# A two-layer recurrent/attention kernel: opening rearranged, and another fixed order of steps in its five engine plans

## The reference

```python
xn = _layernorm(x)
s = _L0_attn_ref(xn, ...)            # a Mamba block: in_proj, causal conv of 4 taps, x_proj, dt, a scan over time
                                     # with 16 states per channel, out_proj; then layernorm, gelu MLP 256-1024-256
g = _silu(_L0_ffn_ref(xn, ...))      # FP4 (blocks of 16) quantize/dequantize of activations and weights, gated MLP
x = x + s * g
xn = _layernorm(x)
s = _L1_attn_ref(xn, ...)            # attention over the batch dimension (two entries), 16 heads of 16
g = _silu(_L1_ffn_ref(xn, ...))      # three blocks: linear - layernorm - gelu - linear, plus residual; weights are
                                     # 4-bit values times scales, plus a low-rank product (LoRA)
x = x + s * g
```

## Time and profile before

| | us |
|---|---|
| median of 3 runs (1772.78 to 1775.84) | 1775.19 |
| the profiled execution's own time | 1773.16 |
| its span | 1771.1 |
| PE busy | 1542.6 |
| DVE busy | 1560.9 |
| ACT busy | 1436.5 |
| POOL busy | 1255.8 |

### The profile page before, as it was taken

One profiled execution on the slowest core, in us unless ns is written; L12 is line 12 of the kernel. 1 busy time (PEld: TensorE's weight loads), 2 busy tenths in 40 slices (PEclk: granted clock), 3 DMA queues, 4 the chain that ended last, 5 costly groups with the idle time before them and its releaser, 6 DMA issues.

```text
span 1771.1 us, 26229 instructions
## 1 busy us (share of the span) xinstructions
PE 1542.6 (87%) x7512; PEld 1161.8 (66%) x7512; DVE 1560.9 (88%) x2887; ACT 1436.5 (81%) x3076; POOL 1255.8 (71%) x1314
## 2 busy tenths in 40 slices
PE   2576888989899999989999899989899999999875
PEld 1254666767677777767676677767676767677654
DVE  3959999999999999999999999989999999989811
ACT  1376788889898989899898989889898988888632
POOL 2656767677777868687777868687777869687522
PEclk8687899999999999999999999999999999989987
DMA  7111111111111112111111111112111111111100
GB/s 177 49 48 56 52 49 48 54 43 50 53 61 43 54 49 58 51 49 61 37 61 49 48 50 65 42 53 56 37 60 49 48 60 55 40 57 48 31 0 12
DMA packets 68452, 91.58 MB, mean 52 GB/s; under 512 B 15742, under 2 KB 34758, under 8 KB 68310
## 3 DMA queue, kind: packets, MB, share of 16 engines
q1 hardware_dynamic: 68310, 89.91, 16.9%
HBM read 85.17 MB, written 4.72 MB: 51 GB/s over the span
## 4 chain that ended last, share of the span: by engine, by line
POOL 26%; PE 25%; DVE 20%; ACT 14%; issue 12%; DMA 1%; SPq 0%; POOLq 0%; ACTq 0%; DVEq 0%
PE bank L338 10%; POOL drive L795 10%; PE bank L454 6%; DVE unit L959 5%; POOL wide L844 3%; DVE hc L966 3%; PE y_ps L364 2%; POOL wide L849 2%; POOL wide L846 2%; ACT unit L570 2%; ACT hx L549 1%; DVE xc L991 1%; ACT ops L536 1%; PE bank L325 1%; ACT L536 1%
## 5 line engine op out<-in xcount | busy, mean ns | idle before, releaser
L795 POOL TENSOR_TENSOR drive<-wx,rows 128x1024 f32<-128x1024 f32 x256 | 603.6, 2358 | 157.1 <-DVE unit L959 81.9
L959 DVE TENSOR_TENSOR_SCAN unit<-unit,drive 128x512 f32<-128x512 f32 x512 | 616.5, 1221 | 35.7 <-POOL drive L802 25.6
L570 ACT ACTIVATE unit<-dt,aneg 128x254 f32<-128x254 f32 x1024 | 441.8, 468 | 8.0
L966 DVE TENSOR_TENSOR hc<-unit,rows 128x512 f32<-128x512 f32 x512 | 340.6, 683 | 5.6
L364 PE MATMUL y_ps<-ident,hc 128*128 128x128 f32 x2048 | 278.6, 282 | 62.6 <-DVE hc L966 62.6
L364 PEld LDWEIGHTS y_ps<-ident,hc 128*128 128x128 f32 x2048 | 242.1, 145 | 116.2 <-DVE hc L966 75.4
L338 PE MATMUL bank<-w_l,ops 128*128 128x256 f32 x768 | 195.7, 399 | 15.0 <-DVE xc L994 8.9
L338 PEld LDWEIGHTS bank<-w_l,ops 128*128 128x128 f32 x768 | 146.0, 197 | 66.1 <-DVE xc L994 20.5
L570 ACT ACT_TABLE_LOAD x109 | 139.8, 1283 | 1.9
L579 ACT ACTIVATE carry<-unit 128x4 f32<-128x4 f32 x512 | 79.2, 169 | 68.5 <-DVE unit L973 63.9
L454 PE MATMUL bank<-ops,w_f 128*128 128x256 f32 x512 | 115.8, 385 | 11.2 <-ACT ops L536 11.2
(11 more groups left out here) (229 smaller groups left out, 3132.4 us busy)
## 6 DMA issues: line engine op xcount, KB each, us to landing
rows<-rows_scratch SPq DMA_DIRECT2D x256, 256.0 KB, 3.3
x_t<-in_L_attn_x_dram SPq DMA_DIRECT2D x16, 256.0 KB, 3.9
xs<-in_L_attn_x_dram SPq DMA_DIRECT2D x16, 256.0 KB, 3.5
out_dram<-xs SPq DMA_DIRECT2D x16, 256.0 KB, 2.2
w_f<-in_L_attn_ffn_w_dram SPq DMA_DIRECT2D x2, 1024.0 KB
ops<-in_L_ffn_qweights_dram SPq DMA_DIRECT2D x1, 1536.0 KB, 15.6
w_in<-in_L_attn_in_proj_w_dram SPq DMA_DIRECT2D x1, 1024.0 KB, 5.3
hq_t<-attn_in_proj_weight_dram SPq DMA_DIRECT2D x1, 768.0 KB
```

The source lines that it names most:

```text
L570: last = a_.activation(u[:, k * TOK:(k + 1) * TOK].rearrange("p (b t) -> p b t", b=B)[:, :, 1:TC], dt[p][:, g, :].rearrange("p (b t) -> p ...
L795: g_.tensor_tensor(drive[n % 2][:, :, :].rearrange("p (g b) t -> p g b t", b=B), wx[p][:, :, :].rearrange("p g (b t) -> p g b t", b=B), ro ...
L959: v.tensor_tensor_scan(u[:, :], u[:, :], d, 0.0, ALU.mult, ALU.add).then_inc(S["scan_done"], 1)
L966: v.tensor_tensor(hc[n % NPROD][:, 4 * half:4 * half + 4, :].rearrange("p (g b) t -> p g b t", b=B), unit_of(ch, n, half)[:, :].rearrange( ...
```

## The change

1. Nine small loads leave SP's queue and are issued by ACT, on a semaphore of their own, `small_in`; ACT waits for it instead of `front_in`, PE for both.
2. On DVE the lora dequantization moves from behind `round_(1)` to behind `step_of(0)`, ahead of `conv1`.
3. The gate turns are grouped by weight (4 of gate, 4 of up, then down), and PE waits for each weight's `unscale` alone.
4. The five plans hold the same steps in another order. The text looks wholly different because the period's start is put elsewhere on ACT, DVE and SP; aligned, between 15 of SP's 20 and 80 of DVE's 119 steps keep their sequence.

```diff
         load_front = [
             (w_in[:, :, :], in_proj_w.rearrange("(k p) n -> p k n", p=P)),
+        ]
+        load_small = [
             (g1c[:, :], ln1_g.rearrange("(k p) -> p k", p=P)),
...
-        for half in range(2):
-            for k in range(KD):
-                for wi, dst in ((0, w_g), (1, w_u)):
+        for wi, dst in ((0, w_g), (1, w_u)):
+            for half in range(2):
+                for k in range(KD):
...
+                    for dst, src in load_small:
+                        act.dma_start(dst, src).then_inc(small_in, 16)
                 act.wait_ge(c_done, 8)
-                act.wait_ge(front_in, 16 * len(load_front))
+                act.wait_ge(small_in, 16 * len(load_small))
...
-                pe.wait_ge(w_out_done, 3)
                 for n, (dst, parts) in enumerate(gate_turns):
+                    pe.wait_ge(w_out_done, 1 + min(n // 4, 2))
...
                 step_of(0)
-                dve_step(dve, "conv1", 0)
-                round_(0)
-                scale(2)
-                step_of(1)
-                round_(1)
                 dve.wait_ge(lora_in, 16 * len(load_lora))
                 v.tensor_scalar(l_raw, q_raw, 1.0 / 7.5, -1.0, ALU.mult, ALU.add).then_inc(lora_deq, 1)
...
                                 .to_broadcast([P, NLIN * KD * D // QB, QB]), ALU.mult).then_inc(lora_deq, 1)
+                dve_step(dve, "conv1", 0)
+                round_(0)
+                scale(2)
+                step_of(1)
+                round_(1)
                 step_of(2)
```

More of the change, by code:

```diff
@@ L75 @@
 PE_PLAN = """
[L76 to L79, removed]
+    b0a-- kv-- xp sum8- q-- dt0 b0T-- hqT0- dt1 sum9- b0b-- v1-- sum10- sum11- h1T-- hqT1- ctxT-- hqT2- b1a--
+    sum12- b2b--- sum13- dn- b1T-- sum14- sum15- ao-- xqT skip ygT0- ygT1- g00 sum0 g01 op- u00 u01 sum1 g10
@@ L80 @@
+    sum2 b1b-- g11 u10 u11 u2T- sum3 h2T-- f10- sum4 f11- f12- f13- uT+ b2a-- sum5 f2- b2T-- xi0+ sum6 xi1+ z0+
+    xn1T- xi2+ xi3+ sum7 z1+
 """
 ACT_PLAN = """
[L82 to L85, removed]
@@ L86 @@
-    f13- exp6b out5b u+ exp7a b2n-- out6a exp7b out6b exp8a out7a exp8b b2g-- tap0+ tap1+ hn- z0+ xn1- tap2+
-    tap3+ z1+ out7b out8a xc0+ xc1+ exp9a exp9b out8b exp10a b0n- kv- xp+ out9a out9b exp10b exp11a dt0+ out10a
-    exp11b hq0 b0g- aexp- dt1+ out10b v1- dtexp+
+    exp11b- dt0 b0g-- aexp-- hq0- dt1 v1-- dtexp out10b- exp12a- out11a- exp12b- out11b- exp13a- h1-- hq1-
+    out12a- exp13b- out12b- hq2- ctx-- dtln out13a- exp14a- out13b- exp14b- exp15a- first out14a- exp15b- b1n--
+    out14b- exp0a gatec--- gatem- b1g-- out15a- exp0b xq out15b- s1-- exp1a out0a yg0- exp1b yg1- out0b exp2a
@@ L89 @@
+    out1a exp2b g00 g01 out1b exp3a out2a out2b exp3b exp4a opn- g10 xn+ g11 out3a out3b exp4b u2- exp5a out4a
+    exp5b h2-- out4b exp6a f10- f11- xhf+ f12- f13- usave out5a exp6b out5b u+ exp7a out6a exp7b out6b b2n--
+    exp8a out7a exp8b b2g-- tap0+ tap1+ hn- z0+ tap2+ xn1- tap3+ xc0+ out7b out8a exp9a z1+ xc1+ exp9b out8b
+    exp10a b0n- out9a exp10b xp+ out9b kv- exp11a out10a
 """
 POOL_PLAN = """
-    drive14- drive15- b1-- arg fix0 drive0 xout fin--- drive1 drive2 hb1-- drive3 fix1 f+ drive4 op- drive5 j0in
@@ L92 @@
-    hb2-- drive6 s0b- drive7 b2-- drive8 j0out j1in x1- drive9 drive10 diff- j1out b0- hb0- drive11 xin+ drive12
+    drive14- arg drive15- fix0 b1-- drive0 xout fin--- drive1 drive2 f+ fix1 drive3 op- drive4 hb1-- drive5 j0in
+    s0b- hb2-- drive6 j0out drive7 b2-- j1in drive8 x1- drive9 drive10 diff- j1out b0- xin+ drive11 hb0- drive12
     drive13 log+
@@ L95 @@
 DVE_PLAN = """
[L96 to L102, removed]
+    scan14b- hc14a- hc14b- clr14a- scan15a- wx clr14b- hc15a- scan15b- hc15b- xround clr15a- clr15b- yg- scan0a
+    hc0a clr0a scan0b hc0b scan1a clr0b hc1a scan1b clr1a scan2a hc1b hc2a clr1b clr2a scan2b op- hc2b ug0 clr2b
+    scan3a scan3b hc3a hc3b clr3a scan4a clr3b h2-- hc4a scale0 ug1 scan4b hc4b clr4a scan5a clr4b hc5a scan5b
+    clr5a scale1 round0 hc5b scan6a hc6a clr5b b2s-- scan6b hc6b clr6a scan7a clr6b scan7b hc7a hc7b clr7a
+    xscale+ clr7b x1- scan8a conv0+ scan8b hc8a hc8b clr8a conv1+ round1 b0s- scan9a clr8b hc9a scan9b clr9a
+    scan10a hc9b clr9b hc10a clr10a scan10b scan11a score- scan11b hc10b hc11a f++ attn- clr10b h1- clr11a hc11b
+    scan12a clr11b hc12a scan12b clr12a hc12b scan13a clr12b scan13b hc13a clr13a b1s- hc13b clr13b dt+ scan14a
 """
 SP_PLAN = """
-    rows8- rows11- load+ rows10- rows12- rows13- wr rows14- rows15- rows0 rows1 rows3 rows2 store--- rows4
-    again- rows6 rows5 rows9 rows7
+    rows5-- rows7-- again--- rows8-- rows11-- load rows9-- rows10-- rows12-- rows13-- wr- rows14-- rows15--
+    rows1- rows0- rows2- rows4- rows3- store---- rows6-
 """
@@ L208, in program @@
         S = {name: sem(name) for name in PER}
-        front_in, lora_in, gate_in, rest_in = (sem(n) for n in ("front_loaded", "lora_loaded", "gate_loaded", "rest_loaded"))
+        front_in, small_in, lora_in, gate_in, rest_in = (
+            sem(n) for n in ("front_loaded", "small_loaded", "lora_loaded", "gate_loaded", "rest_loaded"))
         c_done, unit_zero, small_done = (sem(n) for n in ("const_ready", "unit_zero", "small_done"))
@@ L1274, in turn_copy @@
                     nc.scalar.activation(dst, src, ACT.Copy).then_inc(turn_out, 1)
+                with nc.allow_non_contiguous_dma(reason="vectors laid one element a partition, once"):
+                    for dst, src in load_small:
+                        act.dma_start(dst, src).then_inc(small_in, 16)
                 act.wait_ge(c_done, 8)
-                act.wait_ge(front_in, 16 * len(load_front))
+                act.wait_ge(small_in, 16 * len(load_small))
                 for name in FRONT["ACT"][:FRONT["ACT"].index("xp")]:
@@ L1310, in _ @@
                 pe.wait_ge(front_in, 16 * len(load_front))
+                pe.wait_ge(small_in, 16 * len(load_small))
                 for name in FRONT["PE"][:FRONT["PE"].index("xp")]:
```

## The result

| | before | after |
|---|---|---|
| median of six runs, us | 1773.1 (1771.4 to 1775.8) | 1779.95 (1778.1 to 1780.8) |
| ratio | | 1.0036, 95% interval 1.0023 to 1.0049 |
| profiled execution, us: time, span | 1773.2, 1771.1 | 1780.8, 1779.0 |
| mean granted clock of TensorE | 0.943 | 0.938 |

What follows compares the result with a forecast made beforehand. No engine is full; the order of hand-overs between engines sets the period. From 1773.16, less 15 for the opening and 2 for the steady order, 1756.2, plus 2.0 for the median: 1758, own range 1749 to 1766, wider range 1741 to 1771.

Steps and rivals of the forecast that it cites:

- Opening: Everything before the loop's first gate turn ends: the loop starts 15 us earlier, with ends of 11.4 and 17.
- the 0 and the 6.4 of the two ends: Small loads issued by ACT: limits on how much earlier gate weights land, 6.4 us if transfers were free; 2.0 taken.
- The lora block: DVE's lora dequantization, moved ahead of conv1 where POOL is idle: 5.2 us instead of 8.5, 3.3 less.
- The folds take 72.57 to 93.83, 21.2: PE's folds in the opening: same 21.2 us as before, only starting earlier, at 57.3.
- log to x1 and b0n: First part of a steady period: small waits shrink, -0.3 up to drive0, -0.3 around op, 0 from f1 to x1.
- POOL's wait before xout: Steady period, drive0 to fin: DVE ends xround about 0.8 sooner, so this wait shrinks from 1.93 to 1.1.
- x1 to log: +0.4: Last part of a period: ACT's two added table loads of 1.28 mostly replace waits, costing 0.4 us a period.
- The long periods can come and go with any order: +-4 in all: Periods of 100.05 at clock 0.95: may appear or vanish with any order, within 4 us over the run.
- my -0.2: Sum of the new steady order's effects: -0.2 us a period, taken as -2 for some 15 periods.
- C: Rival: ACT full from tap3 to dtexp, two new table loads count whole, +2.4 a period, 1796 us; chance 0.07.
- B: Rival: the order eats the opening's gain, ACT 1 us late at b0n, +1 a period, 1775 us; chance 0.10.
- D: Rival: the opening keeps little, folds wait on something else or log runs slow, 1766 us; chance 0.12.

Runs made afterwards that it cites:

- open_only: The changed kernel with all five orders of before put back, so only the new opening is left: 1760.8 us (0.9935 of before).
- fold runs: Two filler or moved-sum9 variants of the changed kernel, with ACT copying opening folds 0 and 1 ahead of dtexp, fold 2 ahead of dtln: 1756.1 and 1754.0 us.
- gap_z1: The changed kernel with sum9 ahead of hqT0 on PE, and z1 and xc1 back ahead of exp9a on ACT: 1758.8 us (0.9924 of before).
- pe_fill: The changed kernel, orders kept, with PE computing b0T's transposes three times to fill its idle time before hqT0: 1754.5 us (0.9893 of before).
- oldorder_fill: The old orders with the new opening, plus 8 useless transposes on PE in the idle time before dt0: 1751.5 us (0.9884 of before).
- pe_v1: The changed kernel with v1 moved on PE directly behind hqT0, ahead of dt1, sum9 and b0b: 1789.0 us (1.0093 of before).
- pe_gap: The changed kernel with sum9 moved on PE ahead of hqT0, v1 staying behind b0b: 1759.2 us (0.9927 of before).
- pe_v1gap: The changed kernel with sum9 moved ahead of hqT0 and v1 ahead of dt1 on PE: 1757.2 us (0.9910 of before).
- fill_half: The changed kernel, orders kept, with PE computing b0T's transposes twice, filling part of the idle time before hqT0: 1756.2 us (0.9910 of before).
- fill_warm: The changed kernel with b0T's transposes tripled, ACT's earlier opening fold copies, and 32 useless PE transposes before the lora loads' wait: 1753.2 us (0.9893 of before).

## Why the prediction was wrong

- **Opening, right in kind, 15 forecast, 12.3 measured** (open_only). Gate weights forecast at 26.1, measured 25.1: 2.9 sooner than before, between the 0 and the 6.4 of the two ends. The lora block was forecast at 5.2, measured 5.1; DVE's last preparation ended at 87.5, as forecast. PE was late: first fold 57.3 forecast, 58.3 measured; the folds 21.2 forecast, 23.7 measured; the turns up to the loop's start 9.2 forecast, 10.6 measured. The step that failed is "The folds take 72.57 to 93.83, 21.2": it counted PE alone and not who empties its two buffers, the wait of 3.35. For the turns, the granted clock in them was 0.50 in after and 0.72 before. What each is worth in the median is not shown, as the fold runs scatter too much.
- **log to x1 and b0n, right:** -0.2 forecast, -0.2 to -0.6 read. opn came at 1007.7 (forecast 1008), 3.1 sooner after `log` than before; f1 kept 0.65 of it and x1 0.6, where the forecast had 0.3. ACT had no idle time from tap3 to b0n. POOL's wait before xout did not shrink (1.93, not 1.1), at no cost.
- **"x1 to log: +0.4", the step that failed.** It priced ACT's table loads (gap_z1: nothing) and did not walk PE's order there, where hqT0 moved from ahead of q to three places behind it, onto q's bank. That new wait of 0.92 costs little in itself: in pe_fill useless work takes its place, and the period is 98.69. What it cost is the clock behind it, which made v1, ACT's copy of it and `log` late: 14.75 from b0n to `log` instead of 13.30 in the period shown.
- **"The long periods can come and go with any order: +-4 in all", the term that was mis-sized.** I had read the 0.95 in the earlier trace rows as a scatter with no owner. It has one: in before, q behind the idle 1.07 ahead of `dt0`, in four of thirteen periods. Order decides it. The slow clock costs 3.8 a run in the old order (open_only against oldorder_fill, thirteen periods) and 25.9 in the new one (after against pe_fill); the difference is +22, over five times the bound of 4.
- **A likeness that is luck.** With the clock cured the new orders give 98.69 a period against the 98.99 of before, which looks like my -0.2, and 1754.5 looks like my 1758. But 98.69 is free of slow stretches and 98.99 is not. With both cured the orders differ by 0.03 (98.69 and 98.66), so the -0.2 was not borne out.
- **Slips in the working, without weight.** Fifteen periods of -0.2 are -3, not -2. The first of the thirteen full periods starts at 274.41, not 274.60. The ten shorter ones lie between 98.46 and 99.07, so they do not repeat to within 0.1.
- **The rivals.** C (table loads, 1796) had the right sign and the wrong mechanism. B, "+1 a period", had the nearest size, 1775, and no mechanism. D (1766) did not happen. None was about the clock.

By the Trainium skill (TensorE: Matmul & The Clock Gate, section A second HAM failure mode: psum-queue depth-cycling) a kernel that goes through PSUM banks in turn can idle briefly and often enough between groups of matmuls for the clock to swing between its levels. That agrees with dt1, sum9 and b0b here, and it was the rule to weigh against this change. The same page of the Trainium skill has the clock rise with sustained work (section What's actually happening); no run here shows it in the folds, 0.50 through 17.7 us of after (64.34 to 82.01) in which PE is shown busy.

## What to carry to other kernels

When steps move on PE, find for every product which earlier one holds its bank and who reads that last; then look at what runs behind the idle time, not at the idle time alone. If the same matmuls have two durations in one profile, look for what stands ahead of the slow ones before calling it scatter. And test it with useless work in the gap: it changes no order and no dependency, so if the kernel gets faster and the granted clock there is back at 1.00, the clock was the cause. A move of a step, as in pe_v1, changes several waits at once and does not show that.

## What the runs showed of the hardware that I had not expected

- Idle times of about 1 us on PE are followed by half clock at some places and not at others: 0.92 to 0.94 before hqT0 in all thirteen periods of after, but the same 0.93 there in pe_v1 in only five of thirteen; 1.07 before dt0 (before) in four of thirteen; 1.02 before b0b in two of thirteen (pe_gap) and five of thirteen (pe_v1gap); 0.49 before hqT0 (fill_half) in none. What sets the difference was not found.
- PE shown as busy doesn't raise the clock by itself: folds, each with products of 32 rows, took 1.77 each at 0.50, ten in a row behind the pause of 3.35 (after) and eleven in a row with no pause directly ahead of them (fill_warm, where the clock fell from 1.00 to 0.50 at 61.7, within the first fold). Folds with all 128 rows in use weren't tried.
- A granted clock of 0.50 does not always cost time: in pe_fill it fell in nine of thirteen periods in their first quarter, and these are no longer than the others.
